# Expert stages of a fused attention, recurrence and mixture-of-experts kernel: engines take their work two slots at a time instead of one

## The reference

```
x = x + attention_a(layernorm(x))     # 16 heads of 8, positional mask, MLP 128 -> 512 -> 128
x = x + ffn(layernorm(x))             # mixture of experts
x = x + recurrence_b(layernorm(x))    # gated recurrence in log space over a sequence
x = x + ffn(layernorm(x))             # the same mixture, the same weights
```

```
probs = softmax(x @ router_w.T); keep the top 2 per row, normalise them to sum 1
g = einsum('nd,edf->nef', x, gate_w) + gate_b
u = einsum('nd,edf->nef', x, up_w) + up_b
h = silu(g) * u
expert_out = einsum('nef,efd->ned', h, down_w) + down_b
y = einsum('ne,ned->nd', probs, expert_out)
```

## Time and profile before

| what | us |
|---|---|
| median of 3 runs | 1462.38 (1460.31 to 1465.81) |
| span of the profiled execution | 1622.8 |
| own time of the profiled execution, beside its span | not among the listed times |
| first expert stage in the profile (first transpose to the next phase) | about 263 |
| second expert stage in the profile | about 262 |

### The profile page before, as it was taken

How to read it: one execution, slowest core, us unless ns; L and a number is a source line. 1 busy time by engine, 2 the same in 40 slices (tenths; PEclk the granted TensorE clock), 3 DMA queues, 4 the chain that set the end, 5 groups by cost and what they waited for, 6 DMA issues and landing times. The chain is left out here.

```text
span 1622.8 us, 37888 instructions
## 1 busy us (share of the span) xinstructions
PE 1206.8 (74%) x11717; PEld 1014.2 (62%) x11717; DVE 1149.5 (71%) x3828; ACT 943.0 (58%) x2002; POOL 980.7 (60%) x1152
## 2 busy tenths in 40 slices
PE   3779998888888888972688788476766357887850
PEld 1557777776777777752688787355555257877850
DVE  5379998888888888864555555388888645555538
ACT  2478888887888888841444444266666334444420
POOL 4245687777777777676255555438788735555540
PEclk9599999999999999996789898799899679998875
DMA  7121111111111111131222222112222132222228
GB/s 206 53 76 47 43 58 55 56 56 57 57 57 57 56 57 57 36 116 52 77 75 77 80 77 71 59 51 71 77 80 67 41 90 77 76 77 74 77 72 283
DMA packets 100819, 120.94 MB, mean 75 GB/s; under 512 B 17945, under 2 KB 80721, under 8 KB 100369
## 3 DMA queue, kind: packets, MB, share of 16 engines
q1 hardware_dynamic: 69600, 75.85, 15.9%
q0 software_dynamic: 17280, 35.95, 6.5%
q10 hardware_dynamic: 13744, 6.75, 1.5%
HBM read 49.45 MB, written 44.46 MB: 58 GB/s over the span
## 5 line engine op out<-in xcount | busy, mean ns | idle before, releaser
L1096 DVE TENSOR_TENSOR ebuf<-score_banks,region 128x768 f32<-128x768 f32 x256 | 243.8, 952 | 40.4 <-PE score_banks L809 34.8
L1337 ACT ACTIVATE region<-ebuf 128x768 f32<-128x768 f32 x256 | 215.4, 858 | 21.8 <-DVE ebuf L1096 21.8
L1315 ACT CAST copied<-max_banks 128x768 bf16<-128x768 f32 x256 | 205.4, 802 | 29.6 <-PE max_banks L797 27.3
L1755 POOL DMA_INDIRECT choice_rows<-first_yo,first_xg x142 | 136.7, 963 | 134.4 <-DVE first_yo L1875 100.0
L1755 POOL DMA_INDIRECT choice_rows<-second_yo,second_xg x142 | 137.3, 967 | 126.8 <-DVE second_yo L1875 92.4
L1625 POOL DMA_INDIRECT expert_rows<-d_rows,a_d_index x128 | 131.7, 1029 | 42.5 <-issue 30.8
L2171 POOL DMA_INDIRECT expert_rows<-d_rows,z_d_index x128 | 131.6, 1028 | 38.4 <-issue 32.1
L1831 ACT ACTIVATE first_silu<-first_bgu,first_biases 128x256 f32<-128x256 f32 x142 | 63.2, 478 | 131.6 <-PE first_bgu L1784 63.0
L1831 ACT ACTIVATE second_silu<-second_bgu,second_biases 128x256 f32<-128x256 f32 x142 | 63.1, 477 | 126.2 <-issue 61.3
L1514 POOL TENSOR_TENSOR rs<-arg,neghalf 128x4 f32<-128x4 f32 x32 | 37.1, 1161 | 137.8 <-DVE arg L1028 137.8
L1867 DVE SCALAR_TENSOR_TENSOR second_hT<-second_bgu,second_biases,second_silu 128x256 f32<-128x256 f32 x142 | 64.1, 478 | 74.9 <-ACT second_silu L1831 45.1
(11 more groups left out here) (333 smaller groups left out, 4386.0 us busy)
## 6 DMA issues: line engine op xcount, KB each, us to landing
region_r<-region_r SPq DMA_DIRECT2D x192, 128.0 KB
first_xg<-expert_rows SPq DMA_DIRECT2D x71, 132.0 KB
second_xg<-expert_rows SPq DMA_DIRECT2D x71, 132.0 KB
z_rows<-choice_rows SPq DMA_DIRECT2D x32, 256.0 KB
c_rows<-choice_rows SPq DMA_DIRECT2D x16, 512.0 KB
out<-xres ACTq DMA_DIRECT2D x16, 256.0 KB
choice_rows<-first_yo,first_xg POOLq DMA_INDIRECT x142
choice_rows<-second_yo,second_xg POOLq DMA_INDIRECT x142
```

Of the source, the lines that this page charges most:

```text
L1096: nc.vector.tensor_tensor(ebuf[:, half_of_ebuf(c, j), :, :], score_banks[:, :, 0:BK], bias32[:, plain(j), :], ALU.add).then_inc(scores_fre ...
L1315: nc.scalar.copy(copied[:, 2 * j:2 * j + 2, :], max_banks[:, :, 0:BK]).then_inc(maxed_free, 1)
L1337: nc.scalar.activation(p32[:, j % 4, :, :], ebuf[:, half_of_ebuf(c, j), :, :], ACT.Exp).then_inc(exped, 1)
L1755: pool.indirect_dma_start(choice_dram, bass.IndirectOffsetOnAxis(ap=xg[:, i % G, t, E:E + 1].bitcast(I32), axis=0), yo[:, i % 4, t, :], No ...
```

## The change

The unit of the order becomes the pair of slots ("duo"), and all engines run through the same cycles n. In cycle n

- TensorE does `down` of pair n-1, `transpose_x` of pair n+2, `gate_up` of pair n+1;
- ScalarE `high` of pair n+1, `silu` of pair n, `upper_weights` of pair n+2;
- VectorE `take_y` of pair n-2, `low` of pair n+1, `hidden` of pair n, and then the copies of biases and lower weights of pair n+2, split off from `low`.

The rings of `whi` and `wlo` grow from two to four, that of the silu results from two halves to four, and the row buffers `xg` from 8 to 12. The banks and the rings of `xhi`, `xlo`, `hT` and `yo` stay. `experts_around` is replaced by `reader`, which keeps one packed word per reader; VectorE has two of them. The passes, copies, sums and DMAs of a slot are the same as before.

```diff
@@ -1712,7 +1712,8 @@
     NE, EF, E, ST = s.NE, s.EF, s.E, s.TURNS
     NF = EF // P
-    G = 8
+    G = 12
+    DUOS = (ST + 1) // 2
     expert = w["expert"]
     assert NE == 8 and NF == 2
     with phase(nc) as (ctx, new_sem):
@@ -1727,8 +1728,8 @@
         xg = sb("xg", [P, G, 2, s.ROW])
         xhi, xlo = sb("xhi", [P, 2, 2 * P], F32R), sb("xlo", [P, 2, 2 * P], F32R)
-        whi, wlo = sb("whi", [P, 2, 2 * EF], F32R), sb("wlo", [P, 2, 2 * EF], F32R)
-        act_ = sb("silu", [P, 2, 2 * P])
+        whi, wlo = sb("whi", [P, 4, 2 * EF], F32R), sb("wlo", [P, 4, 2 * EF], F32R)
+        act_ = sb("silu", [P, 4, 2 * P])
         biases = sb("biases", [P, 4, 2 * NF])
         hT = sb("hT", [P, 4, NF, 2 * P])
         yo = sb("yo", [P, 4, 2, E])
@@ -1739,11 +1740,23 @@
             sem("xT_full"), sem("hi_done"), sem("lo_done"), sem("gu_full"), sem("silu_done"), sem("hid_done"),
             sem("y_full"), sem("y_done"), sem("biases_ready"), sem("upper_weights_ready"), sem("lower_weights_ready"))
-        def experts_around(engine, i):
-
-            k = max(i // 4 - 1, 0)
-            word = engine.value_load(expert[0:1, k:k + 1], min_val=0, max_val=NE ** 8 - 1)
-            return lambda j: (word >> (3 * (j - 4 * k))) & (NE - 1)
+        def duo(n):
+            return [i for i in (2 * n, 2 * n + 1) if 0 <= i < ST]
+
+        CYCLES = range(-2, DUOS + 2)
+
+        def reader(engine):
+
+            words = {}
+
+            def of(i):
+                k = i // 4
+                if k not in words:
+                    words.clear()
+                    words[k] = engine.value_load(expert[0:1, k:k + 1], min_val=0, max_val=NE ** 8 - 1)
+                return (words[k] >> (3 * (i - 4 * k))) & (NE - 1)
+
+            return of
         with nc.Block() as block:
             @block.gpsimd
@@ -1759,6 +1772,8 @@
             @block.tensor
             def _(pe):
+                e_down = reader(pe)
+
                 def transpose_x(i):
                     pe.wait_ge(arrived[i % G], 16 * (i // G + 1))
                     if i >= 2:
@@ -1769,7 +1784,7 @@
                 def gate_up(i):
-                    wh, wl = whi[:, i % 2, :], wlo[:, i % 2, :]
+                    wh, wl = whi[:, i % 4, :], wlo[:, i % 4, :]
                     pe.wait_ge(wh_ready, i + 1)
                     pe.wait_ge(wl_ready, i + 1)
                     pe.wait_ge(lo_done, i + 1)
@@ -1795,21 +1810,18 @@
                                                     start=(f == 0), stop=(f == NF - 1))
                     last.then_inc(y_full, 1)
-                for i in range(ST):
-                    if i % 4 == 0:
-                        e = experts_around(pe, i)
-                    transpose_x(i)
-                    if i >= 3:
-                        down(i - 3, e(i - 3))
-                    if i >= 1:
-                        gate_up(i - 1)
-                down(ST - 3, e(ST - 3))
-                gate_up(ST - 1)
-                down(ST - 2, e(ST - 2))
-                down(ST - 1, e(ST - 1))
+                for n in CYCLES:
+                    for i in duo(n - 1):
+                        down(i, e_down(i))
+                    for i in duo(n + 2):
+                        transpose_x(i)
+                    for i in duo(n + 1):
+                        gate_up(i)
             @block.scalar
             def _(act):
+                e_weights = reader(act)
+
                 def high(i):
                     act.wait_ge(xT_full, i + 1)
                     if i >= 2:
@@ -1818,45 +1830,48 @@
                 def upper_weights(i, e):
-                    if i >= 2:
-                        act.wait_ge(gu_full, i * NF - 2)
-                    nc.scalar.copy(whi[:, i % 2, :], w["hi"][:, bass.ds(e, 1), :].rearrange("p a f -> p (a f)")).then_inc(wh_ready, 1)
+                    if i >= 4:
+                        act.wait_ge(gu_full, i * NF + (NF - 4 * NF))
+                    nc.scalar.copy(whi[:, i % 4, :], w["hi"][:, bass.ds(e, 1), :].rearrange("p a f -> p (a f)")).then_inc(wh_ready, 1)
                 def silu(i):
                     act.wait_ge(b_ready, i + 1)
                     for f in range(NF):
                         act.wait_ge(gu_full, i * NF + f + 1)
-                        if i >= 1:
-                            act.wait_ge(hid_done, i * NF + (f + 1 - NF))
-                        nc.scalar.activation(act_[:, f, :], bgu[i % 2 * NF + f][:, 0:2 * P], ACT.Silu,
+                        if i >= 2:
+                            act.wait_ge(hid_done, i * NF + (f + 1 - 2 * NF))
+                        nc.scalar.activation(act_[:, i % 2 * NF + f, :], bgu[i % 2 * NF + f][:, 0:2 * P], ACT.Silu,
                                              bias=biases[:, i % 4, f:f + 1]).then_inc(silu_done, 1)
                 nc.scalar.activation(act_[:, 0, 0:1], ident[:, 0:1], ACT.Silu)
-                for i in range(ST):
-                    if i % 4 == 0:
-                        e = experts_around(act, i)
-                    upper_weights(i, e(i))
-                    high(i)
-                    if i >= 1:
-                        silu(i - 1)
-                silu(ST - 1)
+                for n in CYCLES:
+                    for i in duo(n + 1):
+                        high(i)
+                    for i in duo(n):
+                        silu(i)
+                    for i in duo(n + 2):
+                        upper_weights(i, e_weights(i))
             @block.vector
             def _(dve):
-                def low(i, e):
+                e_weights, e_bias = reader(dve), reader(dve)
+
+                def low(i):
+                    dve.wait_ge(hi_done, i + 1)
+                    nc.vector.tensor_tensor(xlo[:, i % 2, :], bx[i % 2][:, 0:2 * P], xhi[:, i % 2, :].bitcast(F32),
+                                            ALU.subtract).then_inc(lo_done, 1)
+
+                def lower_weights(i, e):
                     if i >= 4:
                         dve.wait_ge(hid_done, i * NF + (NF - 4 * NF))
                     nc.vector.tensor_copy(biases[:, i % 4, :], w["bias"][:, bass.ds(e, 1), :].rearrange("p a f -> p (a f)")
                                           ).then_inc(b_ready, 1)
-                    if i >= 2:
-                        dve.wait_ge(gu_full, i * NF - 2)
-                    nc.vector.tensor_copy(wlo[:, i % 2, :], w["lo"][:, bass.ds(e, 1), :].rearrange("p a f -> p (a f)")).then_inc(wl_ready, 1)
-                    dve.wait_ge(hi_done, i + 1)
-                    nc.vector.tensor_tensor(xlo[:, i % 2, :], bx[i % 2][:, 0:2 * P], xhi[:, i % 2, :].bitcast(F32),
-                                            ALU.subtract).then_inc(lo_done, 1)
+                    if i >= 4:
+                        dve.wait_ge(gu_full, i * NF + (NF - 4 * NF))
+                    nc.vector.tensor_copy(wlo[:, i % 4, :], w["lo"][:, bass.ds(e, 1), :].rearrange("p a f -> p (a f)")).then_inc(wl_ready, 1)
                 def hidden(i):
@@ -1865,7 +1880,7 @@
                     for f in range(NF):
                         dve.wait_ge(silu_done, i * NF + f + 1)
                         nc.vector.scalar_tensor_tensor(hT[:, i % 4, f, :], bgu[i % 2 * NF + f][:, 2 * P:4 * P],
-                                                       biases[:, i % 4, NF + f:NF + f + 1], act_[:, f, :], ALU.add, ALU.mult
+                                                       biases[:, i % 4, NF + f:NF + f + 1], act_[:, i % 2 * NF + f, :], ALU.add, ALU.mult
                                                        ).then_inc(hid_done, 1)
                 def take_y(i, e):
@@ -1875,18 +1890,15 @@
                     nc.vector.tensor_tensor(yo[:, i % 4, :, :], by[i % 2][:, 0:2 * E].rearrange("p (t d) -> p t d", d=E),
                                             w["downb"][:, bass.ds(e, 1), :].broadcast_to([P, 2, E]), ALU.add).then_inc(y_done, 1)
-                for i in range(ST):
-                    if i % 4 == 0:
-                        e = experts_around(dve, i)
-                    low(i, e(i))
-                    if i >= 3:
-                        take_y(i - 3, e(i - 3))
-                    if i >= 1:
-                        hidden(i - 1)
-                take_y(ST - 3, e(ST - 3))
-                hidden(ST - 1)
-                take_y(ST - 2, e(ST - 2))
-                take_y(ST - 1, e(ST - 1))
+                for n in CYCLES:
+                    for i in duo(n - 2):
+                        take_y(i, e_bias(i))
+                    for i in duo(n + 1):
+                        low(i)
+                    for i in duo(n):
+                        hidden(i)
+                    for i in duo(n + 2):
+                        lower_weights(i, e_weights(i))
             @block.sync
             def _(sp):
@@ -1894,7 +1906,7 @@
                     if i >= G:
                         sp.wait_ge(xT_full, i - G + 1)
-                        sp.wait_ge(stored[i % 4], 32 * (i // 4 - 1))
+                        sp.wait_ge(stored[i % 4], 32 * (i // 4 - G // 4 + 1))
```

## The result

After the change the kernel takes 1482.5 us (median of 4 runs, 1479.65 to 1484.49); before, 1462.5 us (4 runs, 1460.31 to 1465.81). The ratio is 1.0135 with a 95% interval of 1.0117 to 1.0154: slower, by 20 us, with an interval of 17 to 22.5 us.

The account below looks back on a forecast made before the run. TensorE was taken as full at 2.545 us per slot, GpSimd nearly so at 2.52. Filling, 7.5 us in each of two stages, added 15 us to 1462.4: 1477.4 us. Range 1448 to 1494 us, likeliest 1472 to 1482.

Parts of the forecast that it names:

- the likeliest case: Expert stages: the change costs only the later start of each stage, 1472 to 1482 us; chance 0.53.
- a timed slot takes about 2.55 us: Expert stages: without halts TensorE is full at 2.545 us per slot, GpSimd nearly so at 2.52.
- The 137 us of halts: Both expert stages: idle stretches, together 137 us, belonging mostly to the recorded execution, against 160 us of span above the median.
- The rival that took them for missing buffers: Expert stages: gaps are real and larger rings absorb them, -53 us net, 1409 us; chance 0.18.
- no gain from fewer changes of kind: TensorE, steady state: fewer switches between kinds of pass give nothing; taken as 0, at most 1.8 us per stage.
- Rings and row buffers: Weight buffers and row loads: four buffers remove a costless wait; twelve row buffers hide the later scatters, with little over.
- Filling: Start of each expert stage: first scatter 7.5 to 8.7 us later than 9.44; 7.5 taken per stage, 15 in all.
- The early-clock case: Start of a stage: TensorE's clock rises at 6.2 us, gate 1 ends at 7.9, first scatter at 16.9 us.
- GpSimd can catch up a little: GpSimd's scatter queue: reason for taking the lower end, 7.5 us per stage; full catch-up 1.8 us per stage.
- VectorE's chain: VectorE, each pair: first output sum ends 0.7 us ahead of the next down product; overrun rival 1498 us, chance 0.12.

Follow-up runs that it names:

- before_again: The kernel before the change, unchanged, profiled a second time: 1464.19 us, with a span of 1462.2 us.
- rings_only: The kernel before with the changed kernel's larger rings (four weight buffers, four silu halves, twelve row buffers), order unchanged: 1462.0 us, ratio 1.0004.
- after_half_scatter: The changed kernel with only the first of each slot's two scatters in the second expert stage: 1471.9 us, ratio 1.0075 to the kernel before.
- half-scatter runs: The changed kernel and the kernel before, each with one of two scatters per slot in the second stage: 1471.9 and 1461.8 us.
- early_sum: The changed kernel with VectorE's output sums one pair earlier, behind the hidden sums: 1475.3 us, ratio 1.0094 to the kernel before.
- short_fill: The changed kernel with each stage's first six slots in the order of before, then pairs: 1475.6 us, ratio 1.0090 to the kernel before.
- early_short: The changed kernel with output sums one pair earlier and each stage's first six slots in the old order: 1469.7 us, ratio 1.0052.

## Why the prediction was right

The sign, the place and the mechanism were forecast: a delay of the scatters, paid once in each stage and passed on by GpSimd. The size was forecast a quarter too small, 15 us against 20. The 1482.5 us lie within the stated range, and half a microsecond above the likeliest case's own 1472 to 1482.

**Which execution to believe.** The step from 1622.8 us back to "a timed slot takes about 2.55 us" held: 2.54 to 2.55 in before_again, with one wait of 0.5 us for hT. The 137 us of halts were not in the program. The rival that took them for missing buffers fell twice, since rings_only changed nothing.

**TensorE.** Taken: no gain from fewer changes of kind. Measured: 5.09 us per pair, with some pairs 0.02 to 0.15 longer and one 0.46. Its last gate pass ends 2.5 and 3.0 us later than in before_again, in part from the start (0.8 and 2.2 us by the end of slot 3's gates), in part from these longer pairs.

**Rings and row buffers.** Costed at nothing; rings_only has 1.0004.

**Filling.** The first scatter was put at 16.9 us, or 18.1 with the clock rising late; it came at 17.4 and 18.0. The early-clock case was right in its steps as well. In the first stage of after_half_scatter, whose program is that of after, the clock rose at 6.1 us. (The 6.2 us that the prediction takes from the earlier trace rows cannot be read from those rows; the trace of that execution has 6.3.) There the gates of slot 1 ended at 7.8 (7.9 predicted), those of slots 2 and 3 took from 9.3 to 12.4 (9.3 to 12.3), and the first scatter came at 17.0 (16.9). The gates started at 10.3 above because the clock rose later in that execution.

The kernel before was put at 9.44 from a disturbed execution; undisturbed it is 9.63 and 8.57 in before_again. By these traces the difference is 7.8 and 9.4 us, where I took 7.5. But the 9.4 holds the luck of the clock. Over all stages in their steady order, the first scatter comes at 9.5 us on average in the order of before (nine stages) and at 17.3 in that of after (five, 17.0 to 18.0). The difference is 7.7 us, so this term was right in size.

**GpSimd passes the delay on.** This is where the sum fell short. I took the low end since "GpSimd can catch up a little". It does not: from its first scatter to the end of its last it needs 1.3 and 0.2 us more than in before_again, and on average over the same stages with all scatters 182.0 us in place of 180.9. In the first stage of after the late sums leave it small gaps; in the second its scatters are longer. With the later start this makes 8.9 us per stage (203.0 in place of 194.1), 17.8 in all; the pair of traces shown has 18.7. The other 2 us of the medians' difference are not located; they are within its interval. The half-scatter runs confirm that GpSimd carries most of it.

**VectorE's chain.** Predicted to end 0.7 us ahead of the next down product. From the rows above, the first output sum of the pair ends at 898.29, 0.64 us ahead of TensorE's start at 898.93; its four hidden sums end 2.77 us into the cycle (2.55 predicted). Where a word is loaded on the way the rest is as small as 0.34 us. The chain fits, as forecast, with less room than counted. This order on VectorE was not free: in early_sum the pairs over 5.09 us, 1.0 and 0.5 us a stage, are gone.

**What I called it.** I named the cost "filling the pipeline". The amount was about right, but short_fill shows that the name misleads: with the old filling, two thirds of the loss stayed (by the stages, three quarters), and the trace shows it paid at the change of order. In the middle of the first stage (slots 30 to 39, means), a slot's first scatter starts 7.4 us behind its first gate pass in before_again and 13.5 us in after. Of the 6.1 us between them, 3.5 are the down product, which stands further behind its gates (4.3 and 7.75 us), 2.1 the output sum behind its product (1.8 and 3.9), and 0.5 the wait in GpSimd's queue. So the offset is only in part the sum's own place. It is paid once per stage. early_sum, short_fill and early_short each take back a part of it (7.2, 6.9 and 12.8 of 20 us by the medians, 3.7, 4.2 and 9.3 of 18.7 by the stages); no run takes out the down product's part by itself. The 8 us that early_short still lacks are nearly all in the two gaps of each stage.

## What to carry to other kernels

Where two engines are both nearly full (here TensorE at 2.545 us and GpSimd at 2.52 us per slot), a reordering that leaves the work per slot as it is gained nothing in the middle here, and the time that it put between the first engine and the last was paid once per stage. Count that offset in the steady order, not only in the first slots, and look for the engine that has no time to make it good. Look at more than one execution before a difference of 1 or 2 us at the start of a stage is explained: the clock's rise alone moved it here. And before waits are read as a kernel's own, hold the profiled execution's time against the timed runs: if it is longer by far, profile once more.

## What the runs showed of the hardware

- One execution of the unchanged kernel was recorded at 1622.8 us and another at 1462.2, with 1462 us in timed runs. In the long one, ScalarE and TensorE stand idle at the same time and go on the earlier trace rows; the timed runs are what marks it.
- Eight extra transposes ahead of a stage did not bring TensorE's higher clock sooner: it rose 6.3 and 7.1 us behind the first transpose of the stage. Without them the rise came after 4.3 to 7.0 us in the order of before, and after 6.1 to 8.8 us in the stages that begin with pairs, and the first scatter moved with it (8.57 us with the rise at 4.3, 10.0 with 6.8).
- GpSimd's drain at the barrier behind an expert stage took 7.8 us from its own start with all scatters in the order of before, 10.8 in that of after, and 7.0 and 7.2 with half of the scatters. It ended 2.8 us behind the last scatter's end with all of them and 5.9 with half, so the 0.96 us in the trace are not all that GpSimd has to do for a scatter, or the drain has a cost of its own. No run tells these apart.
